# Attention stage of a graph kernel: index copied in mid-group, slot sums added from PSUM, one row copied out, exponentials read from PSUM

## The reference, cut to what matters

```python
alpha = a_i[dst] + a_j[src] + edge_terms            # 8 heads for each edge
alpha = jnp.where(alpha >= 0, alpha, 0.2 * alpha)
m = segment_max(alpha, dst); e = jnp.exp(alpha - m[dst]); s = segment_sum(e, dst)
msg = xs[src] * (e / (s[dst] + 1e-16))[:, :, None]
out = segment_sum(msg, dst)                          # (6250, 256)
```

## Time and profile before

| | |
|---|---|
| time, median of 3 runs | 9026.64 us (9007.27 to 9045.2) |
| span of the profiled execution | 9513.5 us |
| time of that execution beside its span | none is given apart from the span |
| attention, layer 1 and layer 2 | about 560 to 1880 us and 2380 to 3650 us of the span |
| granted TensorE clock, mean over the span | 0.708 of full speed |
| busy over the span | PE 64%, DVE 52%, ACT 19%, POOL 54% |

### The profile page before, as it was taken

The page is one execution under the profiler, slowest core; times in us unless marked ns, Lnnn a source line. Parts: engine busy times, 40 slices in busy tenths (PEclk is TensorE's granted clock), DMA queues, the critical chain, the costliest instruction groups (busy, mean ns, idle before and its releaser), DMA issues. The chain is left out here.

```text
span 9513.5 us, 114282 instructions
## 1 busy us (share of the span) xinstructions
PE 6103.6 (64%) x21566; PEld 4079.9 (43%) x21567; DVE 4907.6 (52%) x10800; ACT 1764.1 (19%) x5802; POOL 5094.9 (54%) x4638
## 2 busy tenths in 40 slices
PE   4557777766777775746555578955555566666660
PEld 2245555544555553545555543423222344343430
DVE  4256677765777777753333332133333554444447
ACT  0223333312333331210000001100000122222221
POOL 0057677601777773036666610047666468888880
PEclk7666777668777776755555558976666788888885
DMA  1463333313333332221111123433232346666665
GB/s 28 149 176 102 98 103 106 99 33 125 107 106 104 106 107 57 60 67 24 23 24 23 24 52 122 138 96 89 88 88 88 102 55 68 68 69 69 68 69 168
DMA packets 556641, 796.06 MB, mean 84 GB/s; under 512 B 97181, under 2 KB 430798, under 8 KB 555215
## 3 DMA queue, kind: packets, MB, share of 16 engines
q0 software_dynamic: 271168, 487.56, 25.4%
q1 hardware_dynamic: 258318, 280.98, 9.7%
q10 hardware_dynamic: 27092, 26.85, 1.1%
HBM read 543.23 MB, written 251.81 MB: 84 GB/s over the span
## 5 line engine op out<-in xcount | busy, mean ns | idle before, releaser
L588 POOL DMA_INDIRECT at_x<-table,at_idx x1680 | 1922.6, 1144 | 643.6 <-issue 525.9
L2211 POOL DMA_INDIRECT acc<-sc_rows,sc_idx x832 | 1353.2, 1626 | 298.4 <-DMA acc<-sc_rows,sc_idx 186.6
L660 PE MATMUL at_psO<-at_x,at_main 128*128 128x273 f32 x3328 | 1322.5, 546 | 3.4 <-issue 2.1
L1626 POOL DMA_INDIRECT conv_x<-conv_table,conv_idx x840 | 844.1, 1005 | 515.2 <-DVE conv_prod L1718 276.0
L1679 PE MATMUL rel_psO<-rel_x,rel_hot 128*128 128x257 f32 x1664 | 653.1, 534 | 616.4 <-issue 375.6
L1626 POOL DMA_INDIRECT rel_x<-rel_table,rel_idx x840 | 836.1, 995 | 392.7 <-issue 222.4
L718 ACT COPY at_sums<-at_psO 128x273 f32<-128x273 f32 x1664 | 629.3, 388 | 1804.9 <-PE at_psO L660 1194.8
L660 PEld LDWEIGHTS at_psO<-at_x,at_main 128*128 128x128 f32 x3328 | 798.4, 260 | 254.2 <-issue 61.1
L2251 PE MATMUL sc_psR<-gated,sc_pick 128*128 x1664 | 597.0, 456 | 448.2 <-ACTq L2289 444.6
L1679 PE MATMUL conv_psO<-conv_msg,conv_hot 128*128 128x64 f32 x1664 | 448.4, 433 | 581.6 <-issue 373.1
L826 DVE TENSOR_TENSOR agg<-agg,at_sums 128x273 f32 x1664 | 733.6, 441 | 43.9 <-DVE agg L826 3.8
(11 more groups left out here) (397 smaller groups left out, 9098.7 us busy)
## 6 DMA issues: line engine op xcount, KB each, us to landing
at_place<-places SPq DMA_DIRECT2D x212, 256.0 KB
rel_table<-rt_rows SPq DMA_DIRECT2D x50, 1024.0 KB
at_x<-table,at_idx POOLq DMA_INDIRECT x1680
acc<-zeros ACTq DMA_DIRECT2D x4, 6553.5 KB
la_t<-acc SPq DMA_DIRECT2D x40, 642.5 KB
conv_attr<-in_attr_T SPq DMA_DIRECT2D x840, 6.0 KB
conv_x<-conv_table,conv_idx POOLq DMA_INDIRECT x840
rel_x<-rel_table,rel_idx POOLq DMA_INDIRECT x840
```

The costliest lines, as they stand in the source:

```text
L588: pool.indirect_dma_start(x[b][:, j, 0:TABW], None, d.table[0:NR, :], bass.IndirectOffsetOnAxis(ap=idx[b][:, j:j + 1], axis=0)).then_inc(x ...
L660: nc.tensor.matmul(psO[j % BANKS][:, 0:AGG], main[b % 2][:, j, :], x[b][:, j, 0:AGG], start=True, stop=True).then_inc(o_ready, 1)
L1626: pool.indirect_dma_start(x[b][:, j, 0:WIDE], None, table, bass.IndirectOffsetOnAxis(ap=idx[b][:, j:j + 1], axis=0)).then_inc(x_ready[b], 16)
L2211: pool.indirect_dma_start(d.acc[k][0:NR + P, :], bass.IndirectOffsetOnAxis(ap=idx[b][:, j:j + 1], axis=0), rows[b % 2][:, j, :], None, com ...
```

## The change

Four edits, all in `phase_attention`. The row numbers of the next group are copied between the fourth and the fifth gather of this one. DVE adds slot sums straight from PSUM, and ACT copies only partition 0 of each slot's sums, for `carry`. An eighth PSUM tensor `psE` takes a second copy of the exponentials, which the messages read. DVE's order in `period` is new: four adds of group g itself (slots 0 to 3) and the four last of group g-1. `add` still waits for `copied`, and PE's slot sums now wait for `acc_done` too.

```diff
-        sums = [sb(f"sums{b}", [P, GROUP, AGG]) for b in range(2)]
+        row0 = [sb(f"row0{b}", [1, GROUP, AGG]) for b in range(2)]
+        psE = ps("psE", [P, GROUP, H])
...
+                def index(g, b, turn):
+                    if not (isinstance(turn, int) and turn == 0):
+                        pool.wait_ge(x_ready[b], turn * (16 * GROUP))
+                        pool.sem_inc(idx_pass, 1)
+                    nc.gpsimd.tensor_copy(idx[b][:], m.src_slot[:, bass.ds(g * GROUP, GROUP)]).then_inc(idx_ready, 1)
...
-                    nc.gpsimd.tensor_copy(idx[b][:], m.src_slot[:, bass.ds(g * GROUP, GROUP)]).then_inc(idx_ready, 1)
                     pool.wait_ge(idx_ready, g + 1)
                     for j in range(GROUP):
+                        if j == GROUP // 2 and not last:
+                            index(g + 1, (b + 1) % SETS, turn + 1 if b == SETS - 1 else turn)
                         pool.indirect_dma_start(x[b][:, j, 0:TABW], ...
...
                     pe.wait_ge(copied, i + 1)
+                    pe.wait_ge(acc_done, i + 1)
                     nc.tensor.matmul(psO[j % BANKS][:, 0:AGG], main[b % 2][:, j, :], x[b][:, j, 0:AGG], ...
...
                     act.wait_ge(shift_ready, g + 1)
+                    act.wait_ge(rhs_ready, g * (GROUP // 2))
+                    nc.scalar.activation(psE[:], shifted[:], ACT.Exp).then_inc(ex_ready, 1)
                     nc.scalar.activation(x[b][:, :, D:D + H], shifted[:], ACT.Exp).then_inc(ex_ready, 1)
...
                     act.wait_ge(o_ready, i + 1)
-                    act.wait_ge(acc_done, i + 1)
-                    nc.scalar.copy(sums[b % 2][:, j, :], psO[j % BANKS][:, 0:AGG]).then_inc(copied, 1)
+                    nc.scalar.copy(row0[b % 2][:, j, :], psO[j % BANKS][0:1, 0:AGG]).then_inc(copied, 1)
...
-                        dve.wait_ge(ex_ready, g + 1)
+                        dve.wait_ge(ex_ready, 2 * g + 2)
-                    nc.vector.tensor_tensor(v, v, x[b][:, j:j + 2, D:D + H].unsqueeze(3)..., ALU.mult).then_inc(rhs_ready, 1)
+                    nc.vector.tensor_tensor(v, v, psE[:, j:j + 2, :].unsqueeze(3)..., ALU.mult).then_inc(rhs_ready, 1)
...
+                    dve.wait_ge(o_ready, i + 1)
                     dve.wait_ge(copied, i + 1 + BANKS)
-                    dve.wait_ge(acc_done, i + 2 * GROUP)
-                    nc.vector.tensor_tensor(to, to, sums[b % 2][:, j, :], ALU.add).then_inc(acc_done, 1)
+                    dve.wait_ge(acc_done, i + BANKS)
+                    nc.vector.tensor_tensor(to, to, psO[j % BANKS][:, 0:AGG], ALU.add).then_inc(acc_done, 1)
```

More of the change, by code:

```diff
@@ L579, in _, with gather @@
             def _(pool):
-                def gather(g, b, reused):
+                def index(g, b, turn):
[3 more added lines that the diff above has]
+                    nc.gpsimd.tensor_copy(idx[b][:], m.src_slot[:, bass.ds(g * GROUP, GROUP)]).then_inc(idx_ready, 1)
+                def gather(g, b, turn, reused, last=False):
                     if reused:
                         pool.wait_ge(o_ready, (g - SETS + 1) * GROUP)
-                    nc.gpsimd.tensor_copy(idx[b][:], m.src_slot[:, bass.ds(g * GROUP, GROUP)]).then_inc(idx_ready, 1)
                     pool.wait_ge(idx_ready, g + 1)
@@ L587, in gather @@
                     for j in range(GROUP):
+                        if j == GROUP // 2 and not last:
+                            index(g + 1, (b + 1) % SETS, turn + 1 if b == SETS - 1 else turn)
                         pool.indirect_dma_start(x[b][:, j, 0:TABW], None, d.table[0:NR, :],
                                                 bass.IndirectOffsetOnAxis(ap=idx[b][:, j:j + 1], axis=0)).then_inc(x_ready[b], 16)
+                index(0, 0, 0)
                 for b in range(SETS):
-                    gather(b, b, False)
+                    gather(b, b, 0, False)
                 with pool.Fori(1, NTURN) as it:
                     for b in range(SETS):
-                        gather(it * SETS + b, b, True)
-                gather(NG, 0, True)
+                        gather(it * SETS + b, b, it, True)
+                gather(NG, 0, NTURN, True, last=True)
                 pool.wait_ge(x_ready[0], 16 * GROUP * (NTURN + 1))
@@ L613, in _ @@
                         sp.dma_start(d.carry[bass.ds(g * GROUP, GROUP), :].rearrange("(o j) k -> o (j k)", o=1),
-                                     sums[b][0:1, :, :].rearrange("o j k -> o (j k)")).then_inc(row_stored[b], 16)
+                                     row0[b][:].rearrange("o j k -> o (j k)")).then_inc(row_stored[b], 16)
                 load_places(NG, 0)
@@ L752, in _ @@
                 dve.sem_inc(cols_ready, 1)
-                dve.sem_inc(acc_done, 2 * GROUP)
+                dve.sem_inc(acc_done, BANKS)
                 mT_ch = Chain(dve, mT_step, 2)
@@ L814, in messages @@
                     if j == 0:
-                        dve.wait_ge(ex_ready, g + 1)
+                        dve.wait_ge(ex_ready, 2 * g + 2)
                     v = x[b][:, j:j + 2, 0:D].rearrange("p j (h c) -> p j h c", c=C)
-                    nc.vector.tensor_tensor(v, v, x[b][:, j:j + 2, D:D + H].unsqueeze(3).to_broadcast([P, 2, H, C]), ALU.mult).then_inc(rhs_ready, 1)
+                    nc.vector.tensor_tensor(v, v, psE[:, j:j + 2, :].unsqueeze(3).to_broadcast([P, 2, H, C]), ALU.mult).then_inc(rhs_ready, 1)
                 def add(g, b, j, ns):
                     i = g * GROUP + j
+                    dve.wait_ge(o_ready, i + 1)
                     dve.wait_ge(copied, i + 1 + BANKS)
-                    dve.wait_ge(acc_done, i + 2 * GROUP)
+                    dve.wait_ge(acc_done, i + BANKS)
                     to = m.agg[:, bass.ds(ns[j] * AGG, AGG)]
-                    nc.vector.tensor_tensor(to, to, sums[b % 2][:, j, :], ALU.add).then_inc(acc_done, 1)
+                    nc.vector.tensor_tensor(to, to, psO[j % BANKS][:, 0:AGG], ALU.add).then_inc(acc_done, 1)
                 def period(g, b, turn, last_added):
@@ L835, in period @@
                         ns = tiles_of(g - 1)
[L837 to L840, removed]
                     messages(g, b, 0)
+                    if last_added:
+                        add(g - 1, b0, 4, ns)
+                        add(g - 1, b0, 5, ns)
                     logits_1(g1, b1, t1)
-                    add_before(0)
+                    messages(g, b, 2)
                     logits_2(g1, b1)
-                    messages(g, b, 2)
+                    if last_added:
+                        add(g - 1, b0, 6, ns)
+                        add(g - 1, b0, 7, ns)
+                    ns = tiles_of(g)
+                    messages(g, b, 4)
                     logits_3(g1, b1)
-                    add_before(1)
-                    messages(g, b, 4)
-                    add_before(2)
+                    add(g, b, 0, ns)
+                    add(g, b, 1, ns)
+                    messages(g, b, 6)
                     scans(g1, b1, 0)
-                    add_before(3)
+                    add(g, b, 2, ns)
+                    add(g, b, 3, ns)
                     scans(g1, b1, 1)
                     scans(g1, b1, 2)
-                    messages(g, b, 6)
-                    add_before(4)
+                    onehotT(g + 2, b + 2, turn * 2 + (b + 2) // 2)
                     shifts(g1, b1)
[L857 to L860, removed]
                     onehot(g1, b1)
@@ L877, in _ @@
                 ns = tiles_of(NG - 1)
-                for j in range(GROUP):
+                for j in range(GROUP // 2, GROUP):
                     add(NG - 1, SETS - 1, j, ns)
-                dve.wait_ge(acc_done, S + 2 * GROUP)
+                dve.wait_ge(acc_done, S + BANKS)
 def phase_places(nc, m, d, sem):
```

## The result

The changed kernel takes 9597.97 us (9596.57 to 9605.8, four runs) against 9028.4 us (9007.27 to 9045.2) of the kernel before: a ratio of **1.063** [1.0606, 1.0654], 570 us slower. I had forecast 9310 us, and 9500 as the upper end. In the changed kernel's profiled execution span and time nearly agree, so its rows can be set beside the runs directly. The span of before (9513.5 us) could not: outside the two attention layers its trace has 6859 us, that of after 6405 us, and no edit touches that part.

The account below looks back on a forecast made before the run. POOL's gathers were taken to bound the kernel at 12.3 us a group; DVE's new waits make groups 13.8 us against 12.4, 1.4 x 208 = +290 on 9027, about 9310 us, range 8900 to 9500.

Parts of the forecast that it names:

- Slot 1's add: DVE's wait for slot 1's sum and ACT's copy: 1.75 us a group at full clock, 2.8 at half.
- Slot 3's: DVE's add of slot 3 waiting for its sum and copy: none at full clock, 0.25 us at half.
- the clock's share: Fraction of time PE runs at full clock in attention: 44 to 50%, taken as 0.47, not raised by the change.
- The mixture: Attention group time from 11.7 us at full clock and 16.4 at half, weighted by clock share: 13.8 us.
- worse than my mix: PE's idle pulls full clock down to a 0.25 share: 14.9 us a group, 9550 us; within the 0.70.
- Messages for the exponentials: DVE's wait for ACT's exponentials before a group's first message: 0.45 us, 1.4 at half clock.
- The second load of tile numbers: Register load mid-period in DVE's queue: 0.60 us, partly covered by one add, so 0.3 us a group.
- The group before: Attention group time in the unchanged kernel: 12.4 us, from POOL's 12.3 and a little.
- The expected span: Profiled execution of the changed kernel: a span near 9850 us, against 9513.5 us before.
- POOL's terms: POOL's loop of gathers and moved index copy: from 12.3 to 10.6 to 11.2 us a group.
- Gathers remain the bound: Rival: POOL still sets the attention loop at 11.5 us a group, -190 us, 8840 us; chance 0.20.
- Even: Rival: both effects cancel at 12.4 us a group, full clock 80% or shorter waits, 8980 to 9070 us; chance 0.10.

Follow-up runs that it names:

- 1 to 3: On the kernel before: only the index copy moved (8942.77 us), only the exponentials in PSUM (8905.47 us), both together (8759.43 us).
- experiment 4: Kernel before with only DVE's new order, adds still reading the SBUF copy: 9643.18 us, 1.0692.
- experiment 8: Changed kernel with the last messages and all scans ahead of the four adds of the current group: 8846.2 us, 0.9788.
- 5: Changed kernel with two extra unread matmuls a group ahead of `turn_max`: 9224.25 us, 1.0207.
- 10: Changed kernel with one extra unread matmul a group ahead of `turn_max`: 9488.07 us, 1.0515.
- 11: Changed kernel with four extra unread matmuls a group ahead of `turn_max`: 9140.97 us, 1.0101.
- Experiment 9: Kernel of experiment 8 with two extra unread matmuls a group ahead of `turn_max`: 8908.13 us, 0.9858.
- Experiment 6: Changed kernel with ACT's exponentials ahead of the copies of slots 4 and 5 instead of behind them: 9595.13 us, 1.0614.
- experiment 3: Kernel before with both the index copy moved and the second exponentials in PSUM, DVE's order unchanged: 8759.43 us, 0.9706.
- experiment 7: Kernel of Experiment 6 with DVE's add straight behind PE's sum and ACT's copy waiting for the add: 9464.35 us, 1.0478.

## Why the prediction failed in its size

**What held.** Gathers bound the kernel before: the edits that shorten POOL's loop gained 83, 120 and together 266 us (1 to 3). The order puts the adds of the running group in front of the scans, and this costs more than POOL gains: experiment 4 has the loss with the order alone, experiment 8 takes it away by moving the adds behind the scans. DVE stopped waiting for rows, POOL waits once a group, PE waits 2.15 us for the scan ("some 2 us"), gathers take 1.032 us (1.0 to 1.08), ACT's copy 0.38. Slot 1's add was to wait 2.8 us at half clock and waited 2.58. Slot 3's was to wait 0.25 us for ACT's copy; the 0.21 us in the timeline are a wait for slot 2's add, so it is luck that the two numbers are close. The direction, slower at 0.70, was right.

**The term that failed is the clock's share.** The prediction took full clock for 47% of the time with the words "nothing in these rows raises its clock above that of before": it asked only whether the clock might rise. It fell: 0.63 and 0.62 are full for 25%. The mixture then gives 14.9 us a group instead of 13.8, 1.1 x 206 = 227 us. It stood in the text as a case, "worse than my mix", with 14.9 us and 9550 us, and was not made the forecast although the working named its cause, PE's new idle of 2 us. That the clock is a cause and not just a follower of the long loop is shown by 5, 10 and 11: more work on PE, less time, step by step. Experiment 9 shows the limit of the remedy: where PE has no idle time ahead of `turn_max`, the added matmuls cost as much as the clock gives back, or a little more.

The two feed each other: the adds wait for slot sums, PE stands idle behind them, the granted clock falls with this order (0.63 in experiment 4), and at half clock the slot sums come later still. A forecast with today's share of the clock leaves out the second half of that loop. The Trainium skill, page "TensorE: Matmul & The Clock Gate", section "A second HAM failure mode: psum-queue depth-cycling", tells of a bf16 kernel whose PE idled briefly between groups of matmuls so often that its clock swung between two levels. This f32 kernel's trace agrees as far as it goes: two idle stretches of 1.42 and 1.98 us in the group shown, and a granted clock of 1.00 from 1218.6 to 1222.0 us and of 0.50 from 1226.0 to 1230.0.

**The rest of the group, 0.55 us.** Measured over 92 groups, beside the forecast's terms weighted by the share of groups at full clock (14.9 / 11.7 x 0.25 = 32%):

- DVE's own work 908.52 us in the first window, at 15.45 us a group 9.5 (forecast 9.2): +0.3.
- Adds: (341.3 + 46.4 + 30.4) / 92 = 4.5 us (forecast 0.32 x 1.75 + 0.68 x (2.8 + 0.25 + 2.4) = 4.3): +0.2. In it are 0.33 us of adds that wait for the add right in front; four pairs stand adjacent now, one did before. I had not counted these.
- Messages for the exponentials 0.75 (forecast 1.1) and `dst_terms` 0.13 (none): together -0.2. Experiment 6 shows that the two trade with each other.
- The second load of tile numbers 0.46 (forecast 0.3): +0.2.

Together +0.5 of the 0.55. The step between ACT's copy and the add, estimated at 0.25 us, is 0.14 (the copy ends at 1206.97, the add starts at 1207.11), which works the other way and is contained in the second line.

**The group before** was taken as 12.4 us and is 12.7 by the unprofiled time: -0.3, which hid a part of the error. The sum by these corrections: 290 + 227 + 0.55 x 206 - 0.3 x 206 = 568 us, against 570 measured. The expected span (near 9850) came out at 9595.3, because 9513.5 was not a span to compare with. I had put part of its excess of 487 us down to stalls in attention; 454 us of it (6859 - 6405) lay outside.

**POOL's terms.** The moved copy makes the gap between two gathers 0.36 us (1207.50 to 1207.86) instead of 0.30, so it costs 0.06 us, where I had taken 0.2. A gather beside the new DVE stream takes 1.03, inside the bounds. Neither mattered, since POOL didn't bind.

**The rivals.** "Gathers remain the bound" needed the other loop at 11.7 us. It is what happens in experiments 1 to 3, where the order was left alone. It was priced at 11.5 us a group, above the prediction's own 10.6 to 11.2 us for POOL, and so at -190 us; experiment 3, at 11.2 us, gained 266. "Even" needed full clock for 80% of the time; even with four more matmuls the clock was 0.87 and 0.83 and the kernel 1% slower than before.

**What stays open.** How much of the 134 us of experiment 7 belongs to ACT's copy and how much to the adjacent adds is not told apart: their wait in the list fell from 30.4 us to 1.3 in the same edit, though the second of two still starts 0.57 us after the first in its timeline, against 0.63. Nor is it shown why experiment 8, whose gathers are shorter (1019 ns against 1081), stays 87 us above experiment 3; the waits of adds on adds (47.8 us in the layer) and on ACT (52.5) lie in its loop and not in that of 3, which is an argument and not a test. And it is not shown what in PE's work sets its clock. The busy share does not tell it: PE is busy 76% of the first window in the changed kernel (1128.88 of 1480 us, clock 0.63), 77% before (0.72) and 76% in experiment 9 (0.90). In experiment 9 its idle time lies almost all in one stretch of the group, ahead of `turn_logits`, and in the changed kernel in two; no run tests whether that is the reason.

## What to carry to other kernels

Before a consumer is moved from finished work into the running group, list what is queued behind it on its engine and who waits for that: here four adds moved ahead of three scans cost 600 us, and behind them 752 us less. When a change moves TensorE's idle time to a new place in every turn, work out the loop at its half clock first, and take today's share of the clock only if today's idle stays as it is. Matmuls that nobody reads help where PE stands idle anyway; where they delay a product that is waited for, their cost has to be set against the clock. A change of several edits is worth taking apart: the two that shorten the bounding loop gave 3%, and they are the version to keep (experiment 3, 0.9706).

## What the hardware showed that I had not expected

- Matmuls whose result nobody reads made a kernel faster: 374 us with two in each group (a clock of 0.77 instead of 0.63), 457 us with four (0.87 and 0.83). Where they delayed `turn_max` instead of filling idle time, two of them cost 62 us at a clock of 0.90.
- Two adds in a row, the second with a semaphore wait for the first (`acc_done`), start 0.63 us apart (1208.26 and 1208.89), with 0.21 us of it listed as that wait; a message, which has no such wait, follows an add after 0.35 us (1207.11, 1207.46).
- The profiled execution of a kernel can be 487 us longer than its runs, with 454 us of that in stages that the next kernel's trace passes without it. The share that a span takes outside the changed stage is worth a look before the span is used.
